# Linear attention, value sums and one rsqrt chain moved between ScalarE, GpSimd and VectorE in an attention kernel

## The chip, the cores and the metric

One core of a Trainium2 chip runs the whole program. The metric is the time of one execution on the device in microseconds (us).

## The reference, cut to what matters

For each of 32 batches (256 tokens, 128 channels, 16 heads of 8 channels) an input is normalised, turned into q, k and v, and two kinds of attention are mixed. The first keeps only the 12 largest softmax weights of each row and divides by their sum; the second is linear attention on softmax features of q and k.

```
xn = layernorm(x);  q, k, v = heads(xn @ Wqkv.T + bqkv);  q, k = layernorm(q), layernorm(k)
aw  = softmax(q @ k.T / sqrt(8));  aws = aw where aw >= the 12th largest, else 0
o_s = (aws / (aws.sum + 1e-8)) @ v
qf, kf = softmax(q over its 8 channels), softmax(k over its 8 channels)
o_l = (qf @ (kf.T @ v)) / (qf . kf.sum + 1e-6)
o   = sigmoid(alpha) * o_s + (1 - sigmoid(alpha)) * o_l
y   = x + (o @ Wproj.T + bproj) + (xn @ W[idx] + b[idx])
```

## The kernel before, in words

Each engine has an instruction stream of its own, written out by hand; semaphores tie them together. Every stream is a loop `body(it, par, xr)` over `it` from -2 to 33, and in it a loop over eight **units** `u_`. A unit is two heads: four tiles of 128 queries by 256 keys. A batch passes through several iterations: its input is normalised and q and k computed in iteration `it` = batch - 2, their normalisation and the transfer into the layout for the scores happen one iteration later, its eight units follow in its own iteration, and its result leaves two iterations later. So every iteration works for up to five batches at once. The order of the work on an engine is the order of the `if u_ == ...` pieces in its body, and nothing else.

The chain of one unit g is this. TensorE makes the scores (`score_ps`, L816). VectorE takes the nine largest positions by `largest` (L532, eight values a tile into `top`). GpSimd subtracts the maximum (`drop`, L364). ScalarE makes the exponentials `e` and their sum `z` (L717) and those of the eight largest (`e8`, L722). In the next unit VectorE removes these eight (`remove`, L539, reads `e8`) and finds the next eight (`following`, L545). In the unit after that GpSimd compares the tiles of `e` with the threshold (`below`, L386), and ScalarE does the tiles that `POOL_TILES` leaves over (L730). TensorE transposes `e` and masks what lies below (`turn`, L834 and L835), ScalarE copies it out (`kept`, L687), TensorE multiplies by v (`product`, L855), and ScalarE copies this (`oT`, L739). `score_ps` has two buffers, so scores wait for the exponentials two units back.

VectorE has six places for extra work in each unit, called `extra(u_, k)`, between those four removals and four searches:

```
remove(0) extra(0) remove(1) extra(1) following(0) extra(2) remove(2) extra(3)
following(1) extra(4) remove(3) following(2) extra(5) following(3)
```

Two of these extras are divisions of results that TensorE leaves in PSUM. In unit 3 the linear part `work_ps` (L951) is multiplied by the reciprocal `lin_z` of its ninth column (L560, L563) into `lin`. In unit 5 the gathered value sums in `pv_ps` (`sums`, L866) are multiplied by the reciprocal of `den` (L579, L584, L587) into `o_sparse`. `product` of unit 6 writes `pv_ps` again and waits for this.

Two rsqrt chains run on ScalarE (`rsqrt_steps`, Ln, Identity, Exp, Square) with a Newton step on GpSimd (`refine`, three instructions): one on 64 columns for q and k in unit 1, one on two columns for the input in unit 2 (ScalarE, L667 to L673) and unit 4 (GpSimd, L329 to L333, then `x_shift`). The feature exponentials of q and of k are two instructions (L758), because q carries the score scale and k none.

The normalised q and k are split into three bf16 parts, which ScalarE copies out of `work_ps` in unit 4 (L701, L751) and unit 5 (L751, `part` 2). The SP queue writes each part to DRAM as it comes (`part_slots`), waits for all, and loads the slots for the next batch in four DMAs (L274), first those of units 0 to 3. TensorE's scores for unit 0 of the next batch, issued in unit 7, wait for the first two of these.

## Time and profile before

| what | value |
|---|---|
| three runs, median (lowest to highest) | 1230.13 us (1228.34 to 1232.35) |
| the profiled execution, its own time | 1228.88 us |
| its span in the trace | 1226.5 us |
| granted TensorE clock over the span | 0.976 |
| VectorE (DVE) busy | 1187.3 us, 97% |
| ScalarE (ACT) busy | 1086.7 us, 89% |
| GpSimd (POOL) busy | 1083.7 us, 88% |
| TensorE (PE) busy | 962.0 us, 78% |

The busy time of an engine is the union of its instructions, counted from the trace; the durations of neighbouring instructions overlap a little, so the price of one that stands in a row is the distance from its start to the start of the next. The profiled execution's own time is 2.4 us above its span.

### The profile page before, as it was taken

The page shows a single profiled execution, that of the slowest core. Times are in us where ns is not written, and L with a number is a line of the kernel's source. Part 1 is how long each engine was busy: PE and PEld are TensorE (multiplying, and loading weights), DVE is VectorE, ACT ScalarE, POOL GpSimd, SP SyncE. Part 2 cuts the span into 40 slices and gives each one's busy share as a digit, 9 for nine tenths or more (in the row PEclk, how much of TensorE's full clock was granted, in tenths as well). Part 3 has the DMA queues.
Part 4 walks back from the last instruction along what each step waited for, and adds up shares of the span by engine and source line. Part 5 has one row for each costly group of instructions (what it writes and reads, how often), then busy time and mean ns, then how long its engine had stood idle before and what let it go on. Part 6 is the DMA issues. An engine that isn't in the chain of part 4 may idle for free.

```text
span 1226.5 us, 34671 instructions
## 1 busy us (share of the span) xinstructions
PE 962.0 (78%) x8997; PEld 653.9 (53%) x9028; DVE 1187.3 (97%) x4553; ACT 1086.7 (89%) x3626; POOL 1083.7 (88%) x1688
## 2 busy tenths in 40 slices
PE   2577878877788788788787878778887888788786
PEld 1255555555556555565555555555555555555554
DVE  6699999999999999999999999999999999999994
ACT  2498999999999999999999989999999999999984
POOL 4599999999999999999999999999999999999964
PEclk9999999999999999989999999999999999999989
DMA  2122212222221222221222221222222122222110
GB/s 62 48 74 79 83 46 65 61 80 83 83 70 43 67 70 83 83 79 41 71 60 83 83 84 45 66 58 83 83 83 65 50 66 71 83 83 79 38 52 14
DMA packets 165143, 82.78 MB, mean 67 GB/s; under 512 B 7753, under 2 KB 164943, under 8 KB 164946
## 3 DMA queue, kind: packets, MB, share of 16 engines
q1 hardware_dynamic: 164946, 80.56, 22.9%
q8 instruction: 74, 1.21, 0.4%
q14 instruction: 123, 1.01, 0.3%
HBM read 42.78 MB, written 37.75 MB: 66 GB/s over the span
## 4 chain that ended last, share of the span: by engine, by line
DVE 60%; issue 26%; PE 4%; DVEq 4%; POOL 3%; ACT 2%; SPq 0%; DMA 0%; POOLq 0%; ACTq 0%
DVE rest L539 26%; DVE top L532 20%; DVE next L545 8%; DVEq L75 4%; POOL below L386 2%; PE turn_ps L834 1%; DVE o_sparse L587 1%; ACT e L717 1%; DVE lin_z L560 1%; DVE den L584 1%; PE pv_ps L855 0%; PE turn_ps L835 0%; DVE stats L595 0%; PE work_ps L932 0%; DVE den L579 0%
## 5 line engine op out<-in xcount | busy, mean ns | idle before, releaser
L386 POOL TENSOR_SCALAR below<-e,next 128x256 bf16<-128x256 f32 x800 | 725.8, 925 | 0.5 <-issue 0.4
L717 ACT ACTIVATE e<-score_ps,drop 128x256 f32<-128x256 f32 x1024 | 472.9, 481 | 57.1 <-POOL drop L364 53.8
L834 PE MATMUL turn_ps<-ident,e 128*128 128x128 f32 x2048 | 401.0, 289 | 40.6 <-ACT kept L687 17.8
L539 DVE MATCH_REPLACE8 rest<-e 128x256 f32<-128x256 f32 x1024 | 409.7, 402 | 0.0
L545 DVE MAX8 next<-rest 128x8 f32<-128x256 f32 x1024 | 403.1, 406 | 0.6 <-issue 0.3
L835 PE MATMUL turn_ps<-minus_huge,below 128*128 128x128 bf16 x2048 | 380.1, 225 | 0.0
L532 DVE MAX8 top<-score_ps 128x8 f32<-128x256 f32 x1024 | 358.4, 408 | 6.8 <-PE score_ps L816 6.6
L834 PEld LDWEIGHTS turn_ps<-ident,e 128*128 128x128 f32 x2048 | 297.6, 145 | 78.9 <-issue 33.0
L687 ACT ACTIVATE kept<-turn_ps 128x1024 f32<-128x1024 f32 x256 | 267.8, 1046 | 39.3 <-PE turn_ps L835 38.9
L835 PEld LDWEIGHTS turn_ps<-minus_huge,below 128*128 128x128 bf16 x2048 | 222.3, 109 | 0.8 <-issue 0.2
L717 ACT ACTIVATION_READ_ACCUMULATOR e<-score_ps,drop 128x1 f32 x1024 | 217.4, 212 | 0.0
L855 PE MATMUL pv_ps<-kept,v_aug 128*32 128x256 f32 x2048 | 143.2, 399 | 1.2 <-ACT out_sb L763 0.9
L816 PE MATMUL score_ps<-k_slots,q_slots 64*128 64x256 bf16 x1024 | 103.3, 279 | 15.2 <-issue 9.1
L364 POOL TENSOR_TENSOR drop<-top 128x36 f32<-128x36 f32 x256 | 63.2, 247 | 58.0 <-DVE top L532 56.9
L730 ACT ACTIVATE below<-e,next 128x256 bf16<-128x256 f32 x224 | 108.0, 516 | 0.0
L855 PEld LDWEIGHTS pv_ps<-kept,v_aug 128*32 128x32 f32 x2048 | 55.6, 113 | 48.2 <-issue 28.0
L932 PE MATMUL work_ps<-w_qk,xnT 128*128 128x256 f32 x128 | 46.8, 449 | 31.9 <-ACT xnT L779 31.9
L816 PEld LDWEIGHTS score_ps<-k_slots,q_slots 64*128 64x128 bf16 x1024 | 30.8, 94 | 74.9 <-issue 67.2
L539 DVE MATCH_VALUE_LOAD rest<-e 128x8 f32 x1024 | 68.1, 66 | 0.8 <-ACT e L722 0.8
L722 ACT ACTIVATE e<-drop 128x32 f32<-128x32 f32 x256 | 63.3, 247 | 0.0
L866 PE MATMUL pv_ps<-gather,oT 128*128 128x128 f32 x256 | 35.0, 280 | 31.9 <-ACT oT L739 31.9
L951 PE MATMUL work_ps<-kv,qfT 128*128 128x144 f32 x128 | 25.4, 323 | 38.9 <-DVE kv L553 38.9
(156 smaller groups left out, 1333.2 us busy)
## 6 DMA issues: line engine op xcount, KB each, us to landing
part_slots<-part SPq DMA_DIRECT2D x128, 192.0 KB, 2.3
q_slots<-part_slots SPq DMA_DIRECT2D x64, 256.0 KB, 3.3
k_slots<-part_slots SPq DMA_DIRECT2D x64, 256.0 KB, 4.1
part_slots<-part SPq DMA_DIRECT2D x64, 128.0 KB, 1.9
x_sb<-in_L_attn_x SPq DMA_DIRECT2D x32, 128.0 KB, 4.2
x_res<-in_L_attn_x SPq DMA_DIRECT2D x32, 128.0 KB, 4.1
out_y<-out_sb SPq DMA_DIRECT2D x32, 128.0 KB, 4.4
w_ops<-in_L_ffn_W SPq DMA_DIRECT2D x1, 512.0 KB
```

The source lines that it names most:

```text
L386: nc.gpsimd.tensor_scalar(below[:, r, t, :], e[:, r, t, :], next8[:, r, t, TOPK - 9:TOPK - 8], None, ALU.is_lt).then_inc(s["below_pool"], 1)
L532: nc.vector.max(top[:, q, t, 1:9], score_ps[:, q, t // 2, t % 2, :]).then_inc(s["top_ready"], 1)
L539: nc.vector.match_replace(rest[:, t, :], e8[:, (u_ - 1) % 2, t, :], e[:, (u_ - 1) % RING, t, :], REMOVED).then_inc(s["rest_ready"], 1)
L545: nc.vector.max(next8[:, (u_ - 1) % RING, t, :], rest[:, t, :]).then_inc(s["next_ready"], 1)
L687: nc.scalar.activation(kept[:, u_ % 4], turn_ps[:], ACT.Relu).then_inc(s["turn_copied"], 1)
L717: nc.scalar.activation(e[:, u_ % RING, t, :], score_ps[:, u_ % 2, t // 2, t % 2, :], ACT.Exp, bias=drop[:, u_ % 2, t, 0:1], accum_out=z[:, ...
L722: nc.scalar.activation(e8[:, u_ % 2], drop[:, u_ % 2, :, 1:9], ACT.Exp).then_inc(s["e8_ready"], 1)
L730: nc.scalar.activation(below[:, r, t, :], e[:, r, t, :], ACT.Relu, scale=-1.0, bias=next8[:, r, t, TOPK - 9:TOPK - 8]).then_inc(s["below_a ...
L816: last = mm(score_ps[:, v_ % 2, hh, nt, :], q_slots[rows, side, v_, nt * P:(nt + 1) * P], k_slots[rows, side, v_, :], start=True, stop=True)
L834: mm(dst, e[:, r, t, keys], ident[:], start=True, stop=False, is_transpose=True)
L835: last = mm(dst, below[:, r, t, keys], minus_huge[:], start=False, stop=True)
L855: last = mm(pv_ps[32 * j:32 * (j + 1), 0:N], v_aug[:, side, mc, 4 * q + j, :], kept[:, v_ % 4, j % 2, mc, :], start=(mc == 0), stop=(mc == ...
```

## The change

- The linear part is copied from PSUM to SBUF by ScalarE in unit 3 (`lin_raw`, 288 columns), its reciprocal is taken by VectorE in unit 4 from SBUF, and GpSimd multiplies in unit 4.
- The value sums are copied by ScalarE in unit 5 (`sums_sb`, 288 columns). GpSimd makes the denominator in unit 6 (two instructions), VectorE its reciprocal in unit 7, GpSimd multiplies in unit 7. TensorE's `product` of unit 6 now waits for the copy.
- One rsqrt chain of 66 columns in unit 1 takes the place of the two. VectorE's statistics of the input move from unit 1 to unit 0, and the load of the input one iteration ahead.
- q and k both carry 8^(-1/4), so that one exponential of 512 columns makes both features.
- `POOL_TILES` goes from (3, 2, 3, 4, 4, 4, 3, 2) to (3, 2, 4, 3, 4, 3, 3, 2), its first entry being unit 2: GpSimd does one tile more in unit 4, one less in units 5 and 7; ScalarE the reverse.

```diff
 SHARE_MIN = 1e-20
 Z_EPS = 1e-6
-SCORE_SCALE = float(1.0 / np.sqrt(np.float32(D)))
+SIDE_SCALE = float(np.float32(D) ** -0.25)
 UNITS = H // 2
...
 SLOTS_OF = ((slice(0, 3), slice(3, 6), slice(6, 8)), (slice(0, 8, 3), slice(1, 8, 3), slice(2, 8, 3)))
 ROWS = len(SLOTS) * D
-POOL_TILES = (3, 2, 3, 4, 4, 4, 3, 2)
+POOL_TILES = (3, 2, 4, 3, 4, 3, 3, 2)
 POOL_SUM = sum(POOL_TILES)
...
-                if exists(it + 2) and not (isinstance(it, int) and it < 0):
-                    wait_alone(sp, s["xn_ready"], NT * (it + 1), s["waits_passed"])
-                    sp.dma_start(x_sb[:, par], x_t[it + 2]).then_inc(x_loaded[par], 16)
+                if exists(it + 3) and not (isinstance(it, int) and it < -1):
+                    wait_alone(sp, s["xn_ready"], NT * (it + 2), s["waits_passed"])
+                    sp.dma_start(x_sb[:, nxt], x_t[it + 3]).then_inc(x_loaded[nxt], 16)
                 if exists(it - 2):
...
-            def refine(rsqrt, kind, n):
-                v, r, half, out = (rsqrt[:, i] for i in range(4))
-                nc.gpsimd.tensor_tensor(half, half, v, ALU.mult).then_inc(s[kind + "_newton"], 1)
-                wait_alone(pool, s[kind + "_newton"], n + 1, s["waits_passed"])
-                nc.gpsimd.tensor_scalar(half, half, -1.0, 1.5, ALU.mult, ALU.add).then_inc(s[kind + "_newton"], 1)
-                pool.wait_ge(s[kind + "_newton"], n + 2)
-                nc.gpsimd.tensor_tensor(out, r, half, ALU.mult).then_inc(s[kind + "_newton"], 1)
+            def refine(it):
+                lo = 0 if exists(it + 1) else GROUPS
+                hi = GROUPS + NT if exists(it + 2) else GROUPS
+                n = STEPS * (it + 2)
+                v, r, half, out = (rsqrt[:, i, lo:hi] for i in range(4))
+                pool.wait_ge(s["rsqrt_ready"], 2 * (it + 3))
+                nc.gpsimd.tensor_tensor(half, half, v, ALU.mult).then_inc(s["newton"], 1)
+                wait_alone(pool, s["newton"], n + 1, s["waits_passed"])
+                nc.gpsimd.tensor_scalar(half, half, -1.0, 1.5, ALU.mult, ALU.add).then_inc(s["newton"], 1)
+                pool.wait_ge(s["newton"], n + 2)
+                nc.gpsimd.tensor_tensor(out, r, half, ALU.mult).then_inc(s["newton"], 1)
+            def shift(it):
+                n = STEPS * (it + 2)
+                pool.wait_ge(s["newton"], n + 3)
+                nc.gpsimd.tensor_tensor(x_shift[:, 0], moments[:, GROUPS:, 0], rsqrt[:, 3, GROUPS:],
+                                        ALU.mult).then_inc(s["newton"], 1)
+                wait_alone(pool, s["newton"], n + 4, s["waits_passed"])
+                nc.gpsimd.tensor_scalar(x_shift[:, 1], x_shift[:, 0], -1.0, None, ALU.mult).then_inc(s["newton"], 1)
...
+                    if u_ == 6 and exists(it - 1):
+                        wait_alone(pool, s["sums_copied"], it, s["waits_passed"])
+                        nc.gpsimd.tensor_scalar(den[:, 0], z[:, nxt].rearrange("p t h -> p (t h)"), SUM_EPS, None,
+                                                ALU.mult).then_inc(s["den_step"], 1)
+                        pool.wait_ge(s["den_step"], it)
+                        nc.gpsimd.tensor_tensor(den[:, 1], den[:, 0], sums_sb[:, :, D], ALU.add).then_inc(
+                            s["den_ready"], 1)
...
+                    if u_ == 1 and (exists(it + 1) or exists(it + 2)):
+                        refine(it)
...
-                        pool.wait_ge(s["x_rsqrt_ready"], 2 * (it + 3))
-                        n = X_STEPS * (it + 2)
-                        refine(x_rsqrt, "x", n)
-                        pool.wait_ge(s["x_newton"], n + 3)
-                        nc.gpsimd.tensor_tensor(x_shift[:, 0], x_mv[:, :, 0], x_rsqrt[:, 3],
-                                                ALU.mult).then_inc(s["x_newton"], 1)
-                        wait_alone(pool, s["x_newton"], n + 4, s["waits_passed"])
-                        nc.gpsimd.tensor_scalar(x_shift[:, 1], x_shift[:, 0], -1.0, None,
-                                                ALU.mult).then_inc(s["x_newton"], 1)
+                        shift(it)
+                    if u_ == 4 and exists(it):
+                        pool.wait_ge(s["linz_ready"], it + 1)
+                        nc.gpsimd.tensor_tensor(lin[:, par].rearrange("p t (h d) -> p (t h) d", d=D),
+                                                lin_raw[:, :, 0:D],
+                                                lin_z[:].unsqueeze(2).to_broadcast([P, NT * H, D]),
+                                                ALU.mult).then_inc(s["lin_ready"], 1)
...
+                    if u_ == 7 and exists(it - 1):
+                        pool.wait_ge(s["rden_ready"], it)
+                        nc.gpsimd.tensor_tensor(o_sparse[:].rearrange("p t (h d) -> p (t h) d", d=D),
+                                                sums_sb[:, :, 0:D],
+                                                den[:, 2].unsqueeze(2).to_broadcast([P, NT * H, D]),
+                                                ALU.mult).then_inc(s["osp_ready"], 1)
...
-                    if u_ == 3 and k in (1, 3) and exists(it):
-                        w = work_ps[:, 0:NT * H * VA].rearrange("p (t h e) -> p t h e", t=NT, e=VA)
-                        if k == 1:
-                            dve.wait_ge(s["w_lin"], it + 1)
-                            nc.vector.reciprocal(lin_z[:], w[:, :, :, D]).then_inc(s["linz_step"], 1)
-                        if k == 3:
-                            dve.wait_ge(s["linz_step"], it + 1)
-                            nc.vector.tensor_tensor(
-                                lin[:, par].rearrange("p t (h d) -> p (t h) d", d=D),
-                                work_ps[:, 0:NT * H * VA].rearrange("p (g e) -> p g e", e=VA)[:, :, 0:D],
-                                lin_z[:].rearrange("p t h -> p (t h)").unsqueeze(2).to_broadcast([P, NT * H, D]),
-                                ALU.mult).then_inc(s["lin_ready"], 1)
...
-                    if u_ == 5 and 1 <= k <= 4 and exists(it - 1):
-                        w = pv_ps[:, 0:NT * H * VA].rearrange("p (g e) -> p g e", e=VA)
-                        n = 2 * (it - 1)
-                        if k == 1:
-                            dve.wait_ge(s["w_turn"], it)
-                            nc.vector.scalar_tensor_tensor(out=den[:, 0], in0=z[:, nxt].rearrange("p t h -> p (t h)"),
-                                                           scalar=SUM_EPS, in1=w[:, :, D], op0=ALU.mult,
-                                                           op1=ALU.add).then_inc(s["den_step"], 1)
+                    if u_ == 4 and k == 1 and exists(it):
+                        dve.wait_ge(s["lin_copied"], it + 1)
+                        nc.vector.reciprocal(lin_z[:], lin_raw[:, :, D]).then_inc(s["linz_ready"], 1)
+                    if u_ == 7 and k == 1 and exists(it - 1):
+                        dve.wait_ge(s["den_ready"], it)
+                        nc.vector.reciprocal(den[:, 2], den[:, 1]).then_inc(s["rden_ready"], 1)
+                    if u_ == 0 and exists(it + 2):
                         if k == 2:
...
-                            dve.wait_ge(s["den_step"], n + 1)
-                            nc.vector.reciprocal(den[:, 1], den[:, 0]).then_inc(s["den_step"], 1)
-                        if k == 4:
-                            dve.wait_ge(s["den_step"], n + 2)
-                            nc.vector.tensor_tensor(o_sparse[:].rearrange("p t (h d) -> p (t h) d", d=D), w[:, :, 0:D],
-                                                    den[:, 1].unsqueeze(2).to_broadcast([P, NT * H, D]),
-                                                    ALU.mult).then_inc(s["osp_ready"], 1)
-                    if u_ == 1 and exists(it + 2):
-                        if k == 0:
...
+            def rsqrt_steps(it):
+                lo = 0 if exists(it + 1) else GROUPS
+                hi = GROUPS + NT if exists(it + 2) else GROUPS
+                n = it + 2
+                if exists(it + 1):
+                    act.wait_ge(s["ss_ready"], it + 2)
+                if exists(it + 2):
+                    act.wait_ge(s["x_mean"], NT * (it + 3))
+                wait(act, s["newton"], STEPS * n)
+                nc.scalar.activation(log[:, lo:hi], moments[:, lo:hi, 1], ACT.Ln, bias=LN_EPS).then_inc(
+                    s["rsqrt_step"], 1)
+                nc.scalar.activation(rsqrt[:, 0, lo:hi], moments[:, lo:hi, 1], ACT.Identity, bias=LN_EPS).then_inc(
+                    s["rsqrt_ready"], 1)
+                act.wait_ge(s["rsqrt_step"], 2 * n + 1)
+                nc.scalar.activation(rsqrt[:, 1, lo:hi], log[:, lo:hi], ACT.Exp, scale=-0.5).then_inc(
+                    s["rsqrt_step"], 1)
+                act.wait_ge(s["rsqrt_step"], 2 * n + 2)
+                nc.scalar.activation(rsqrt[:, 2, lo:hi], rsqrt[:, 1, lo:hi], ACT.Square,
+                                     scale=float(0.5 ** 0.5)).then_inc(s["rsqrt_ready"], 1)
...
+                    if u_ == 3 and exists(it):
+                        act.wait_ge(s["w_lin"], it + 1)
+                        wait(act, s["lin_ready"], it)
+                        nc.scalar.copy(lin_raw[:].rearrange("p g e -> p (g e)"), work_ps[:, 0:NT * H * VA]).then_inc(
+                            s["lin_copied"], 1)
...
-                            wait(act, s["osp_ready"], it - 1)
+                            wait(act, s["den_ready"], it - 1)
...
+                    if u_ == 5 and exists(it - 1):
+                        act.wait_ge(s["w_turn"], it)
+                        wait(act, s["osp_ready"], it - 1)
+                        nc.scalar.copy(sums_sb[:].rearrange("p g e -> p (g e)"), pv_ps[:, 0:NT * H * VA]).then_inc(
+                            s["sums_copied"], 1)
...
-                        sub = d_sub[:].rearrange("p (t a c) -> p t a c", t=NT, a=2)
-                        for side, dst, factor in ((0, q_exp[:, nxt], 1.0 / SCORE_SCALE), (1, k_exp[:], 1.0)):
-                            nc.scalar.activation(dst, sub[:, :, side, :], ACT.Exp,
-                                                 scale=factor).then_inc(s["dexp_ready"], 1)
+                        nc.scalar.activation(qk_exp[:, nxt].rearrange("p t a c -> p (t a c)"), d_sub[:], ACT.Exp,
+                                             scale=1.0 / SIDE_SCALE).then_inc(s["dexp_ready"], 1)
...
-                        wait(pe, s["osp_ready"], it)
+                        wait(pe, s["sums_copied"], it)
...
-                        wait(pe, s["lin_ready"], it + 1)
+                        wait(pe, s["lin_copied"], it + 1)
```

Names in the rows below: `part` is a bf16 part of q and k, `e` the exponentials, `kept` the masked transpose. **VectorE in unit 5**, before:

```order
L532 MAX top<-score_ps 128x8 [waits scores_ready,drop_ready]
L532 MAX top<-score_ps 128x8 [waits scores_ready] x3
L539 MATCH_REPLACE rest<-e 128x256 [waits e8_ready,next_ready] x2
L579 SCALAR_TENSOR_TENSOR den<-z,pv_ps 128x32 [waits w_turn]
L545 MAX next<-rest 128x8 [waits rest_ready]
L584 RECIPROCAL den<-den 128x32 [waits den_step]
L539 MATCH_REPLACE rest<-e 128x256 [waits e8_ready,next_ready]
L545 MAX next<-rest 128x8 [waits rest_ready]
L587 TENSOR_TENSOR o_sparse<-pv_ps,den 128x256 [waits den_step]
L539 MATCH_REPLACE rest<-e 128x256 [waits e8_ready,next_ready]
L545 MAX next<-rest 128x8 [waits rest_ready] x2
```

and now:

```order
L556 MAX top<-score_ps 128x8 [waits scores_ready,drop_ready]
L556 MAX top<-score_ps 128x8 [waits scores_ready] x3
L563 MATCH_REPLACE rest<-e 128x256 [waits e8_ready,next_ready] x2
L569 MAX next<-rest 128x8 [waits rest_ready]
L563 MATCH_REPLACE rest<-e 128x256 [waits e8_ready,next_ready]
L569 MAX next<-rest 128x8 [waits rest_ready]
L563 MATCH_REPLACE rest<-e 128x256 [waits e8_ready,next_ready]
L569 MAX next<-rest 128x8 [waits rest_ready] x2
```

Three instructions are gone from the unit: the denominator, its reciprocal and the multiplication; the reciprocal comes back in unit 7.

**ScalarE in unit 5, from its exponentials to the v copy of unit 6**, before:

```order
L717 ACTIVATE e,z<-score_ps,drop 128x256 [waits turn_ready,drop_ready]
L717 ACTIVATE e,z<-score_ps,drop 128x256 x3
L722 ACTIVATE e<-drop 128x32
L751 CAST part<-work_ps 128x512 [waits w_rest,next_ready]
L775 ACTIVATE xn<-x_sb,x_shift,x_rsqrt 128x128 [waits w_xT,x_newton]
L775 ACTIVATE xn<-x_sb,x_shift,x_rsqrt 128x128
L687 ACTIVATE kept<-turn_ps 128x1024 [waits turn_ready,pv_ready]
L705 COPY v_aug<-work_ps 128x32x8 [waits w_v_ready]
```

and now:

```order
L731 ACTIVATE e,z<-score_ps,drop 128x256 [waits turn_ready,drop_ready]
L731 ACTIVATE e,z<-score_ps,drop 128x256 x3
L736 ACTIVATE e<-drop 128x32
L744 ACTIVATE below<-e,next 128x256 [waits next_ready]
L760 COPY sums_sb<-pv_ps 128x288 [waits osp_ready,w_turn]
L770 CAST part<-work_ps 128x512 [waits w_rest]
L788 ACTIVATE xn<-x_sb,x_shift,rsqrt 128x128 [waits w_xT,newton]
L788 ACTIVATE xn<-x_sb,x_shift,rsqrt 128x128
L698 ACTIVATE kept<-turn_ps 128x1024 [waits turn_ready,pv_ready]
L719 COPY v_aug<-work_ps 128x32x8 [waits w_v_ready]
```

A `below` tile and the copy of the sums now stand ahead of the last part, of `xn` and of `kept`.

**GpSimd from the start of unit 4 to the start of unit 5**, before:

```order
L364 TENSOR_TENSOR drop<-top 128x36 [waits top_ready,e8_ready]
L386 TENSOR_SCALAR below<-e,next 128x256 [waits next_ready] x3
L329 TENSOR_TENSOR x_rsqrt<-x_rsqrt 128x2 [waits x_rsqrt_ready]
L331 TENSOR_SCALAR x_rsqrt<-x_rsqrt 128x2 [waits x_newton]
L333 TENSOR_TENSOR x_rsqrt<-x_rsqrt 128x2 [waits x_newton]
L402 TENSOR_TENSOR x_shift<-x_mv,x_rsqrt 128x2 [waits x_newton]
L405 TENSOR_SCALAR x_shift<-x_shift 128x2 [waits x_newton]
L364 TENSOR_TENSOR drop<-top 128x36 [waits top_ready,e8_ready]
```

and now:

```order
L372 TENSOR_TENSOR drop<-top 128x36 [waits top_ready,e8_ready]
L402 TENSOR_SCALAR below<-e,next 128x256 [waits next_ready] x4
L340 TENSOR_TENSOR x_shift<-moments,rsqrt 128x2 [waits newton]
L343 TENSOR_SCALAR x_shift<-x_shift 128x2 [waits newton]
L419 TENSOR_TENSOR lin<-lin_raw,lin_z 128x256 [waits linz_ready]
L372 TENSOR_TENSOR drop<-top 128x36 [waits top_ready,e8_ready]
```

The three Newton instructions of the input are gone, one tile and the multiplication of the linear part have come.

## Rows read from the trace of the kernel before

**Rows 1.** Waits (all engines): engine, line, releaser: us in total, times, longest.

```profile
POOL drop L364 <- DVE top L532: 56.9, 99, 6.6
...
DVE den L579 <- PE pv_ps L866: 11.7, 2, 11.0
...
PE score_ps L816 <- issue: 9.1, 13, 1.4
```

**Rows 2.** Stretch of one batch, all engines: busy us (count), clock.

```profile
602.90:639.25 36.35, 28.86 (x283) 19.85 (x283) 36.35 (x141) 33.87 (x114) 33.63 (x53) 1.00 0.25 71
```

**Rows 3.** Timeline, VectorE, starts of units 5 to 0 and extras: start, us, instruction.

```profile
573.99 1.40 DVE L532 MAX8 top<-score_ps 128x8 f32<-128x256 f32 x4
...
576.10 0.17 DVE L579 SCALAR_TENSOR_TENSOR den<-z,pv_ps 128x32 f32<-128x32 f32 x1
576.19 0.41 DVE L545 MAX8 next<-rest 128x8 f32<-128x256 f32 x1
...
577.45 0.40 DVE L587 TENSOR_TENSOR o_sparse<-pv_ps,den 128x256 f32<-128x256 f32 x1
577.78 0.07 DVE L539 MATCH_VALUE_LOAD rest<-e 128x8 f32 x1
...
578.83 1.40 DVE L532 MAX8 top<-score_ps 128x8 f32<-128x256 f32 x4
...
583.25 1.39 DVE L532 MAX8 top<-score_ps 128x8 f32<-128x256 f32 x4
...
587.45 0.73 DVE L532 MAX8 top<-score_ps 128x8 f32<-128x256 f32 x2
```

**Rows 4.** Costliest groups, VectorE: count, busy us, mean ns of one.

```profile
L563 DVE TENSOR_TENSOR lin<-work_ps,lin_z 128x256 f32<-128x256 f32 x32 | 13.0, 407 | 0.0
...
L560 DVE RECIPROCAL lin_z<-work_ps 128x32 f32<-128x32 f32 x32 | 10.9, 341 | 0.0
...
L604 DVE RECIPROCAL k_rec<-k_sum 128x32 f32<-128x32 f32 x32 | 10.5, 328 | 3.8 <-POOL k_sum L415 3.8
```

**Rows 5.** Timeline, GpSimd, units 4 and 5.

```profile
574.30 0.20 POOL L329 TENSOR_TENSOR x_rsqrt<-x_rsqrt 128x2 f32<-128x2 f32 x1
...
575.25 0.20 POOL L402 TENSOR_TENSOR x_shift<-x_mv,x_rsqrt 128x2 f32<-128x2 f32 x1
...
575.84 0.24 POOL L364 TENSOR_TENSOR drop<-top 128x36 f32<-128x36 f32 x1
576.07 3.64 POOL L386 TENSOR_SCALAR below<-e,next 128x256 bf16<-128x256 f32 x4
```

**Rows 6.** Costliest groups, GpSimd.

```profile
L351 POOL TENSOR_TENSOR qkn<-qk_b,beta 128x512 f32<-128x512 f32 x32 | 40.7, 1271 | 0.1
...
L422 POOL TENSOR_TENSOR k_feat<-k_exp,k_rec 128x256 f32<-128x256 f32 x32 | 20.3, 634 | 0.5 <-DVE k_rec L604 0.5
```

**Rows 7.** Timeline, ScalarE, units 4 to 6.

```profile
573.61 0.52 ACT L730 ACTIVATE below<-e,next 128x256 bf16<-128x256 f32 x1
574.01 0.38 ACT L739 COPY oT<-pv_ps 128x256 f32<-128x256 f32 x1
574.26 0.61 ACT L751 CAST part<-work_ps 128x512 bf16<-128x512 f32 x1
...
576.27 0.51 ACT L717 ACTIVATE e<-score_ps,drop 128x256 f32<-128x256 f32 x1
...
578.18 0.65 ACT L751 CAST part<-work_ps 128x512 bf16<-128x512 f32 x1
...
580.34 0.44 ACT L705 COPY v_aug<-work_ps 128x256 f32<-128x256 f32 x1
```

**Rows 8.** Timeline, TensorE, the scores of a unit 0 that came latest.

```profile
732.41 0.60 PE L816 MATMUL score_ps<-k_slots,q_slots 64*128 64x256 bf16 x4 [1.45 <-issue]
```

**Rows 9.** Timeline, VectorE, the unit 0 that needed them.

```profile
733.18 1.43 DVE L532 MAX8 top<-score_ps 128x8 f32<-128x256 f32 x4
```

**Rows 10.** One line, VectorE, within one batch: duration ns min/median/max.

```profile
L539 DVE MATCH_REPLACE8 rest<-e x33: 395/397/407, 566.2 to 602.6; 128x256 f32<-128x256 f32 x33
```

92 lines of the change are left out of this document (38 added, 54 removed).

## The prediction

> **What bounds the kernel now.** Start with the stretch of one batch: 36.35 us from one batch to the next, and VectorE is busy for all 36.35 of them, ScalarE for 33.87, GpSimd for 33.63 [rows 2]. 32 batches of 36.35 are 1163 of the 1226.5 us of the span. Then the waits: GpSimd waits for VectorE's `top` in 99 places, 56.9 us in all, while VectorE itself has one long wait, 11.0 us at the very end [rows 1]. So VectorE sets the pace, and an instruction taken from it shortens every batch, as long as nothing behind it becomes late. The timeline of VectorE gives the unit lengths: unit 5 takes 4.84 (573.99 to 578.83), unit 6 4.42, unit 7 4.20 [rows 3]. The third thing to see is thin cover. TensorE waited 13 times before scores with no engine named, up to 1.4 us [rows 1]. These are unit 0's scores, waiting for the slot loads; in the worst case they start at 732.41 and end at 733.01, and VectorE begins that unit at 733.18 [rows 8, 9]. Today this costs nothing, by 0.17 us.
>
> **What VectorE loses, part by part.** `o_sparse` goes: 577.45 to 577.78 is 0.33 us. `den` goes: 576.10 to 576.19 is 0.09 [rows 3]. `lin` goes; it has the same form and duration (407 ns against 0.40 us) [rows 3, 4], so 0.33. Both reciprocals stay. That of the linear part now reads SBUF; the one that reads PSUM takes 341 ns, one that reads SBUF 328 [rows 4], so 0.01, which I take as 0.4 us over the run. Statistics and their aggregation only change unit. Together 0.33 x 32 for `lin`, 0.42 x 31 for the sums (the last batch's stand in the tail), and 0.4: **24.0 us less**. A batch would take 35.6.
>
> The Trainium skill (VectorE: DVE Perf Modes, "The TRN2 errata") gives VectorE a fixed part of 58 cycles from SBUF and 120 from PSUM at 0.96 GHz. By that the reciprocal would gain 65 ns, an estimate, 2 us over the run instead of 0.4. The trace disagrees in size.
>
> **What GpSimd gets.** In each batch it loses one tile, 3.64 / 4 = 0.91, and three Newton instructions, 574.30 to 575.25 = 0.95 [rows 5]. It gets two multiplications of 256 columns. The nearest row is `k_feat` with 0.63; the upper bound is 1.27, the costliest row of two inputs, which has 512 columns [rows 6]; the lower is 0.33, what VectorE pays. The inputs now step by 9, not 8, but that is close to `k_feat`, so 0.63 each. It also gets two small instructions on 32 columns for the denominator, between 0.2 each (the smallest row) and 0.63; I take 0.7 for both with the wait between them. Sum: 1.96 more, 1.86 less, so +0.1. Of its 36.35 it spends 33.63 busy, about 1.3 in gaps between its own dependent instructions, and the rest waiting for VectorE. 34.9 + 0.1 = 35.0 fits into 35.6. On average GpSimd doesn't bind.
>
> **What ScalarE gets.** Two copies of 288 columns: one of 256 costs 574.01 to 574.26 = 0.25, so 0.28 each. One tile more: 573.61 to 574.01 = 0.40 [rows 7]. It loses the four small activations of the input's chain, each between nothing and the 0.25 of the copy, so 0 to 1.0; with one exponential less I take 0.7 for all of it. Sum: +0.3, 34.2 of 35.6. Also hidden on average.
>
> **Where it gets tight: unit 5.** Place by place, from the start T5 of VectorE's unit 5. Before: GpSimd's `drop` at +1.85 [rows 5], ScalarE's exponentials at +2.28, last `part` at +4.19, v copy at +6.35 [rows 7], unit 0 of the next batch at +13.46 [rows 3]. Now:
> - GpSimd's unit 4 grows by 0.91 + 0.63 - 0.95 = 0.59, VectorE's by 0.25 (the moved reciprocal), so `drop` comes 0.34 later. ScalarE was 0.16 later still than `drop` allowed; a unit 4 without tile leaves it early enough. The exponentials start at +2.48, 0.20 later.
> - Tile and copy of the sums stand ahead of the last `part`: 0.40 + 0.28. It is cast at +5.07, **0.88 later**.
> - Unit 0 comes at +13.04, because unit 5 is 0.64 shorter and unit 7 is 0.22 longer by its reciprocal: **0.42 earlier**.
>
> On the SP queue nothing passes anything, but the last part's two writes and the four slot loads wait for this cast. So the slack between slot loads and unit 0 shrinks by 1.30. In the 13 late cases, read from the two timelines as in the one that is shown, it was 0.17 to 1.36, 11.3 us in sum. 13 x 1.30 - 11.3 = **5.6 us** of new stalls: VectorE waits for unit 0's scores. In the other batches TensorE's scores are done 1.7 ahead, and nothing is lost. The bounds are 0 (the loads get out of each other's way, as the input's load is a batch ahead now) and 11 (as many more cases come into reach).
>
> The second thin place is `product` of unit 6. It waited for `o_sparse`; now it waits for the copy of the sums, which ends at 2.48 + 1.91 + 0.40 + 0.38 = +5.2. From the product to the v copy took 2.3, so v is copied at +7.5 and unit 6's exponentials start at +7.8. They take 2.05 with `e8`, and VectorE removes with `e8` 1.33 after the start of unit 7, at +9.95. Margin 0.1. I put 1 us for the batches that miss it; bounds 0 and 5.
>
> **The tail.** After the last sums the chain was three VectorE instructions, 1.0 us (`den` 0.17, reciprocal 0.33, `o_sparse` 0.40 and two hops). Now it is the copy (0.38), GpSimd twice (0.7), reciprocal (0.33), GpSimd (0.63): 2.1 with its hops. GpSimd ends its tiles one earlier but has a multiplication more. +1.0. At the start the chain that ends last runs over VectorE's setup, unchanged: 0.
>
> **Sum.** 1228.9 (own time of the profiled execution) - 24.0 + 5.6 + 1.0 + 1.0 = **1212.5 us**. The median of the runs, 1230.1, is 0.1% above the profiled one; I leave the number at 1212.5.
>
> **The rivals.**
> - *Nothing stalls:* the slot loads still arrive. 1228.9 - 24.0 + 1.0 = 1206. For it: the input load moved ahead; the late cases are less than half. Against: 13 of them are there already and the cast is later by the sum of rows above.
> - *Unit 6 misses `e8` in every batch.* If ScalarE or TensorE is 0.3 later than worked out, VectorE loses 0.3 x 32 = 9 us more: 1221. For it: a margin of 0.1 on a path of five engines. Against: every price on it stands in a row.
> - *GpSimd becomes the bound, slower than before.* The place is its multiplications with inputs that step by 9. It decides from 35.6 - 35.0 = 0.6 us a batch, and the gain is gone at 1.3, which is where each costs as much as 512 columns (1.27 against 0.63). With the denominator at its upper bound besides (+0.5) a batch takes 36.8: 1228.9 + 0.45 x 32 + 1 = 1244. Against: `k_feat` at 0.63 has a broadcast input too.
> - *GpSimd's reads hold VectorE up.* MATCH_REPLACE takes 395 to 407 ns within one batch [rows 10], in which GpSimd works for 33.63 of 36.35 [rows 2]. If it did hold it up, the new 1.26 a batch would come back as waits of VectorE: 1228.9 - 24 + 40 + 1 = 1246. The rows show nothing like it. The Trainium skill (Perfetto Trace Analysis, "Optimizing Scalar/DVE Operations") warns of just this: both share an SBUF read port, so moving operations between them might not help. The Trainium skill (SBUF — State Buffer, "Who interferes with whom") limits it to VectorE instructions with two SBUF inputs or in a two-port mode; so far the trace agrees, since those of this kernel are not held up.
> - *The change doesn't take work from VectorE:* excluded, the order of instructions shows three fewer a batch.
>
> **How the numbers follow.** Forecast (5 to 12 us of stalls and tail) 0.47; nothing stalls 0.22; `e8` missed 0.16; slower through GpSimd 0.06, through the port 0.02; what I don't see, from no gain to a small loss, 0.07. A measurement of this kernel tells 0.3%, 3.7 us. Faster by more than that: 0.47 + 0.22 + 0.15 = 0.84, since a missed `e8` could take more than I priced; the same 0.01 of that and 0.06 of the unseen, 0.07; slower 0.06 + 0.02 + 0.01 = 0.09. The range goes from 1204 (nothing stalls, tail at nothing) to 1224 (the stalls at both upper bounds); it leaves out 0.2.
>
> **What would show it.** In the changed profile: two copies of 288 columns on ScalarE at about 0.38; VectorE's unit 5 at 4.20; `lin` and `o_sparse` on GpSimd at 0.63; `part` 2 cast 5.1 after T5; a batch of 35.6 where nothing stalls, and VectorE waiting for `score_ps` in some batches. Wrong: multiplications above 0.9; GpSimd no longer waiting for `top`; waits of VectorE for ScalarE's `e8` in every batch; or units of VectorE that grow without a wait.

## The result and the profile after

| | median | runs, lowest to highest |
|---|---|---|
| before | 1229.89 us | 20 runs, 1227.97 to 1232.74 |
| changed | 1222.3 us | 20 runs, 1216.27 to 1228.83 |

The ratio is 0.9939, 95% interval [0.9924, 0.9954]: faster by 0.6%, 7.6 us. Forecast were 1212.5 and a gain of 17. The direction was right and the range (1204 to 1224) holds the time, but less than half of the gain arrived. The profiled execution took 1221.65 us, its span 1219.9.

**The waits of the changed kernel** answer to [rows 1]. Columns: engine, line, releaser, us in total, times, longest.

```profile
PE pv_ps L869 <- ACT sums_sb L760: 55.6, 31, 2.0
POOL drop L372 <- DVE top L556: 52.0, 92, 7.2
...
DVE top L556 <- PE score_ps L830: 12.9, 14, 6.3
DVE den L591 <- POOL den L391: 12.0, 1, 12.0
DVE rest L563 <- ACT e L736: 4.8, 14, 0.6
```

GpSimd still waits for VectorE's `top`, as before. New are the first row, in which TensorE stands before `product` of unit 6 in 31 of the 32 batches, and the last: VectorE waits for ScalarE's `e8`. The `top` row holds 6.3 us at the start of the program; 6.6 us of it lie in the batches.

**One quiet batch**, all engines (busy us and count of PE, PEld, DVE, ACT, POOL, then clock, DMA share, GB/s), beside [rows 2]:

```profile
400.08:435.83 35.75, 28.49 (x279) 19.55 (x278) 35.68 (x138) 33.98 (x114) 33.79 (x53) 1.00 0.25 73
```

35.75, not 35.6: VectorE has 0.07 of idle time by this count, and its first remove of unit 7 comes 0.15 late. **The timeline of VectorE** in it, beside [rows 3]:

```profile
422.63 1.41 DVE L556 MAX8 top<-score_ps 128x8 f32<-128x256 f32 x4
...
426.84 1.41 DVE L556 MAX8 top<-score_ps 128x8 f32<-128x256 f32 x4
...
431.26 1.40 DVE L556 MAX8 top<-score_ps 128x8 f32<-128x256 f32 x4
432.73 0.09 DVE L563 MATCH_VALUE_LOAD rest<-e 128x8 f32 x1
```

Unit 5 takes 4.21 (predicted 4.20), unit 6 4.42. The first remove of unit 7 starts 1.47 after the unit, where it needs 1.33. **ScalarE's timeline**, beside [rows 7]:

```profile
425.10 0.47 ACT L731 ACTIVATE e<-score_ps,drop 128x256 f32<-128x256 f32 x1 [0.55 <-POOL drop L372]
...
427.02 0.52 ACT L744 ACTIVATE below<-e,next 128x256 bf16<-128x256 f32 x1
427.42 0.41 ACT L760 COPY sums_sb<-pv_ps 128x288 f32<-128x288 f32 x1
427.70 0.62 ACT L770 CAST part<-work_ps 128x512 bf16<-128x512 f32 x1
...
430.23 0.37 ACT L719 COPY v_aug<-work_ps 128x256 f32<-128x256 f32 x1 [0.23 <-PE work_ps L935]
430.50 0.48 ACT L731 ACTIVATE e<-score_ps,drop 128x256 f32<-128x256 f32 x1
```

and **TensorE's** `product` behind the copy, then its scores of the next unit 0 (an engine's wait stands in brackets behind its row):

```profile
427.97 1.07 PE L869 MATMUL pv_ps<-kept,v_aug 128*32 128x256 f32 x16 [1.73 <-ACT sums_sb L760]
...
435.22 0.40 PE L830 MATMUL score_ps<-k_slots,q_slots 64*128 64x256 bf16 x4 [0.33 <-issue]
```

From T5 = 422.63, measured (predicted): exponentials +2.47 (+2.48), last part +5.07 (+5.07), copy of the sums ended +5.20 (+5.2), product +5.34 (+5.2), v copy +7.60 (+7.5), exponentials of unit 6 +7.87 (+7.8), VectorE's first remove +10.10 (wanted +9.95). **GpSimd's groups** (count, busy us, mean ns), beside [rows 6]:

```profile
L419 POOL TENSOR_TENSOR lin<-lin_raw,lin_z 128x256 f32<-128x256 f32 x32 | 20.2, 630 | 0.0
...
L438 POOL TENSOR_TENSOR o_sparse<-sums_sb,den 128x256 f32<-128x256 f32 x32 | 20.1, 628 | 0.5 <-DVE den L591 0.5
```

Both multiplications cost what `k_feat` costs, and units 0 to 6 of VectorE have the same lengths in nearly all batches (4.72, 4.21, 4.42, 4.80, 4.41, 4.21, 4.42).

**Where the rest went.** Unstalled, units 6 and 7 take 8.82 together. Over 31 batches they took 16.7 us more than that, read from the starts of VectorE's units. 7.4 of these are waits for `e8`: about 0.15 in most batches, 0.25 to 0.68 in eleven. The other 9.3 stand before unit 0. (The list of waits puts down 4.8 and 6.6; it leaves the smallest out.) In six batches TensorE's scores of unit 0 waited with no engine named, which is the slot loads:

```profile
292.22 0.40 PE L830 MATMUL score_ps<-k_slots,q_slots 64*128 64x256 bf16 x4 [1.07 <-issue]
```

These six are worth 3.5 us. The largest cases, 1.6 us of the two kinds together in each of four batches, show another thing. **TensorE in one of them:**

```profile
572.45 1.07 PE L869 MATMUL pv_ps<-kept,v_aug 128*32 128x256 f32 x16 [1.89 <-ACT sums_sb L760]
...
578.58 1.16 PE L946 MATMUL work_ps<-w_qk,xnT 128*128 128x256 f32 x2
...
581.20 0.40 PE L830 MATMUL score_ps<-k_slots,q_slots 64*128 64x256 bf16 x4
```

**the stretches around it, TensorE** (busy us and count, granted clock, DMA share, GB/s):

```profile
571.00:572.00 1.00, 0.00 (x0) 1.00 0.00 0
572.00:573.00 1.00, 0.55 (x12) 1.00 0.00 0
573.00:574.00 1.00, 1.00 (x15) 0.97 0.21 65
574.00:575.00 1.00, 1.00 (x6) 0.50 0.70 198
...
580.00:581.00 1.00, 1.00 (x4) 0.62 1.10 328
581.00:582.00 1.00, 1.00 (x11) 1.00 0.43 126
```

**and VectorE:**

```profile
575.79 1.43 DVE L556 MAX8 top<-score_ps 128x8 f32<-128x256 f32 x4
577.59 0.09 DVE L563 MATCH_VALUE_LOAD rest<-e 128x8 f32 x1 [0.38 <-ACT e L736]
...
581.79 1.10 DVE L556 MAX8 top<-score_ps 128x8 f32<-128x256 f32 x3 [1.01 <-PE score_ps L830]
```

TensorE stood for 1.89 us, worked again, and then the granted clock fell to 0.50, from 574 to 580.8. That is the lower of its two levels, 1.2 GHz, as the Trainium skill has them (TensorE: Matmul & The Clock Gate, "What's actually happening"; the trace agrees in that it shows 1.00 and 0.50 of the full clock). TensorE, busy in every slice at that level, needs 5.41 us from the start of VectorE's unit 7 to the scores of unit 0, against 3.96 in the quiet batch (435.22 after 431.26), and VectorE waits. Of the 16.7 us, then: 7.4 for `e8`, 3.5 for slot loads, about 5 for scores that come late in batches with a low clock, and 0.8 that I don't assign.

**The tail.** After the last value sums TensorE waits for `o_sparse` before it gathers it. Kernel before, then changed kernel:

```profile
1220.38 0.33 PE L894 MATMUL pv_ps<-ident,o_sparse 128*128 128x128 f32 x1 [1.12 <-DVE o_sparse L587]
```

```profile
1211.94 0.33 PE L908 MATMUL pv_ps<-ident,o_sparse 128*128 128x128 f32 x1 [2.41 <-POOL o_sparse L438]
```

The wait is 1.3 us longer, near the +1.0 of the forecast. But from there to the end of the program it takes 7.98 us instead of 6.15, since the granted clock is 0.52 in this stretch and was 1.00 before. From the start of VectorE's last unit to the end the changed kernel takes 28.5 us, against 25.4.

### The profile page after: what moved, and what is told of

It reads as the page before. It is cut to its first block, busy times and chain, and to the rows that moved or that the text cites. A ratio compares the mean times of both kernels' runs of the same rounds, so it can differ in the third digit from the quotient of the medians.

```text
span 1219.9 us, 34490 instructions
## 1 busy us (share of the span) xinstructions
PE 964.7 (79%) x8997; PEld 659.4 (54%) x9028; DVE 1166.8 (96%) x4457; ACT 1094.1 (90%) x3566; POOL 1090.5 (89%) x1691
## 4 chain that ended last, share of the span: by engine, by line
DVE 33%; ACT 23%; issue 20%; PE 13%; POOL 8%; DVEq 2%; DMA 1%; SPq 0%; POOLq 0%; ACTq 0%
ACT e L731 13%; DVE rest L563 13%; DVE top L556 11%; POOL below L402 6%; DVE next L569 4%; PE pv_ps L869 3%; ACT kept L698 2%; PE work_ps L934 2%; PE turn_ps L848 2%; DVEq L75 2%; ACT below L744 1%; PE work_ps L946 1%; PE turn_ps L849 1%; ACT e L736 1%; PE work_ps L935 1%
## 5 line engine op out<-in xcount | busy, mean ns | idle before, releaser
L402 POOL TENSOR_SCALAR below<-e,next 128x256 bf16<-128x256 f32 x768 | 695.7, 922 | 0.1
L848 PE MATMUL turn_ps<-ident,e 128*128 128x128 f32 x2048 | 399.4, 289 | 34.4 <-ACT kept L698 16.7
L563 DVE MATCH_REPLACE8 rest<-e 128x256 f32<-128x256 f32 x1024 | 419.0, 414 | 0.3 <-issue 0.3
L569 DVE MAX8 next<-rest 128x8 f32<-128x256 f32 x1024 | 412.0, 416 | 0.4 <-issue 0.3
L698 ACT ACTIVATE kept<-turn_ps 128x1024 f32<-128x1024 f32 x256 | 271.1, 1059 | 32.0 <-PE turn_ps L849 31.6
L731 ACT ACTIVATION_READ_ACCUMULATOR e<-score_ps,drop 128x1 f32 x1024 | 228.8, 223 | 0.0
L869 PE MATMUL pv_ps<-kept,v_aug 128*32 128x256 f32 x2048 | 138.9, 389 | 56.9 <-ACT sums_sb L760 55.6
L744 ACT ACTIVATE below<-e,next 128x256 bf16<-128x256 f32 x256 | 128.4, 531 | 0.0
L563 DVE MATCH_VALUE_LOAD rest<-e 128x8 f32 x1024 | 82.2, 80 | 6.0 <-ACT e L736 4.8
L753 ACT COPY oT<-pv_ps 128x256 f32<-128x256 f32 x128 | 51.9, 406 | 1.3 <-PE pv_ps L869 1.3
```

The source lines that it names most:

```text
L402: nc.gpsimd.tensor_scalar(below[:, r, t, :], e[:, r, t, :], next8[:, r, t, TOPK - 9:TOPK - 8], None, ALU.is_lt).then_inc(s["below_pool"], 1)
L563: nc.vector.match_replace(rest[:, t, :], e8[:, (u_ - 1) % 2, t, :], e[:, (u_ - 1) % RING, t, :], REMOVED).then_inc(s["rest_ready"], 1)
L569: nc.vector.max(next8[:, (u_ - 1) % RING, t, :], rest[:, t, :]).then_inc(s["next_ready"], 1)
L698: nc.scalar.activation(kept[:, u_ % 4], turn_ps[:], ACT.Relu).then_inc(s["turn_copied"], 1)
L731: nc.scalar.activation(e[:, u_ % RING, t, :], score_ps[:, u_ % 2, t // 2, t % 2, :], ACT.Exp, bias=drop[:, u_ % 2, t, 0:1], accum_out=z[:, ...
L744: nc.scalar.activation(below[:, r, t, :], e[:, r, t, :], ACT.Relu, scale=-1.0, bias=next8[:, r, t, TOPK - 9:TOPK - 8]).then_inc(s["below_a ...
```

## The experiments

Edits are relative to the changed kernel where nothing else is said. Theory A was: what counts is when `product` of unit 6 starts. Theory B was the one of the prediction: the last part is cast late, and the slot loads with it. Code cuts are marked with `...`.

**The copy of the sums early.** It moves in ScalarE's unit 5 from behind `e8` and the tile to a place ahead of the exponentials, right behind `kept`.

```diff
+                    if u_ == 5 and exists(it - 1):
+                        act.wait_ge(s["w_turn"], it)
+                        wait(act, s["osp_ready"], it - 1)
+                        nc.scalar.copy(sums_sb[:].rearrange("p g e -> p (g e)"), pv_ps[:, 0:NT * H * VA]).then_inc(
+                            s["sums_copied"], 1)
                     if u_ == 3 and exists(it):
...
-                    if u_ == 5 and exists(it - 1):
-                        act.wait_ge(s["w_turn"], it)
-                        wait(act, s["osp_ready"], it - 1)
-                        nc.scalar.copy(sums_sb[:].rearrange("p g e -> p (g e)"), pv_ps[:, 0:NT * H * VA]).then_inc(
-                            s["sums_copied"], 1)
```

> The changed kernel, with ScalarE's copy of the value sums moved from behind unit 5's exponentials and tile to ahead of them, right behind `kept`. Theory A (TensorE's product of unit 6 stands 1.8 us a batch waiting for this copy, and everything behind it, v copy, unit 6's exponentials, the next batch's scores, comes that much later and reaches VectorE in unit 7): the wait of product for sums_sb goes, VectorE's unit 7 goes back from 4.58 to 6.0 us to 4.42, total 1207 to 1211 us, and the runs lie close together. Theory B (the recorded one: the last part is cast too late and the slot loads with it): the part comes only 0.3 us earlier, total 1218 to 1221 us, spread as wide as now.

Measured 1206.71 us (1206.0 to 1209.29), ratio 0.9806 [0.9788, 0.9825]. That is 0.3 below A's range, and 11 below B's. The wait for `sums_sb` is gone from TensorE, and a batch takes what was predicted for one that doesn't stall:

```profile
397.48:433.06 35.58, 31.34 (x282) 21.49 (x281) 35.58 (x138) 33.41 (x110) 33.88 (x53) 0.91 0.26 75
```

This batch has a stretch of low clock too (0.91 on average), and it costs nothing. So low clock by itself is not yet a loss; it becomes one where TensorE's work has no cover left.

**The last part first.** The opposite: the last part's cast goes ahead of the tile and of the copy, which makes the slot loads earlier and the product later.

```diff
+                    if u_ == 5 and exists(it + 1):
+
+                        p = u_ - 3
+                        act.wait_ge(s["w_rest"], 2 * (it + 1) + p)
+                        nc.scalar.copy(part[:, p], work_ps[:].rearrange("p (a n) -> p a n", a=2)).then_inc(
+                            s["part_ready"], 1)
                     if exists(it if u_ >= 2 else it - 1):
...
-                    if u_ in (4, 5) and exists(it + 1):
+                    if u_ == 4 and exists(it + 1):
```

> The changed kernel, with unit 5's cast of the last part moved ahead of the `below` tile and of the copy of the sums; the copy comes 0.5 us later. Theory A: TensorE waits 0.5 us longer, unit 7 grows by that in every batch, total 1232 to 1238 us. Theory B: the slot loads come 0.7 us earlier, the waits for scores go, total 1215 to 1218 us.

Measured 1260.33 us (1259.41 to 1261.91), ratio 1.0240 [1.0221, 1.0258]. Right in sign, but the loss against the changed kernel is 38 us, more than twice what A allowed. Waits of VectorE:

```profile
DVE top L556 <- PE score_ps L836: 41.3, 43, 6.3
...
DVE rest L563 <- ACT e L736: 12.9, 32, 0.6
```

The waits for `e8` explain 15 us; the larger part is the wait for scores, in batches with low clock. This is where the clock became part of the theory.

**The sums back on VectorE.** Copy, denominator and multiplication of the sums are undone; the linear part stays moved.

```diff
-                    if u_ == 7 and k == 1 and exists(it - 1):
...
+                    if u_ == 5 and 1 <= k <= 4 and exists(it - 1):
...
-                        wait(pe, s["sums_copied"], it)
+                        wait(pe, s["osp_ready"], it)
```

> The changed kernel with the value sums divided on VectorE in unit 5 as before (no copy, no GpSimd steps for them); linear part, rsqrt chain, exponential and tiles stay changed. VectorE has 0.42 us a batch more. Theory A: product waits for VectorE's o_sparse, not for ScalarE, no excess in unit 7, total 1230 - 24 + 13 = about 1219 us, and the runs within 3 us of each other. Theory B: the part comes 0.3 us earlier and unit 5 is 0.4 longer, most late batches covered, total 1222 us or more.

Measured 1215.47 us (1214.97 to 1217.02), ratio 0.9872 [0.9853, 0.9892], 3.5 below A's 1219; the narrow spread is as A had it. The half of the change that takes 0.42 us a batch off VectorE makes the program 7 us slower than leaving it out. VectorE's batch is 36.01 here, as the sum has it (36.35 less the 0.33 for `lin`).

**The old table of tiles**, without and with the early copy.

```diff
-POOL_TILES = (3, 2, 4, 3, 4, 3, 3, 2)
+POOL_TILES = (3, 2, 3, 4, 4, 4, 3, 2)
```

> The changed kernel with the tiles shared as before the change (GpSimd 4 in unit 5, 3 in unit 4, 4 in unit 7), so that no tile stands ahead of the copy in unit 5. Theory A: the copy and the product come 0.4 us earlier and unit 7's excess goes, but GpSimd has 0.9 us a batch more (about 35.9 against VectorE's 35.6), total 1212 to 1219 us. Theory B: the part is 0.4 us earlier too, but only the batches with late slot loads gain; with GpSimd's part 1220 to 1226 us. If GpSimd were the bound already, 1240 us or more.

> The early copy with the tiles shared as before the change: GpSimd has one tile, 0.9 us, a batch more, about what the merged rsqrt chain took from it. By the sum of rows GpSimd needs 35.9 a batch against VectorE's 35.6: total 1215 to 1220 us if it is the bound then; 1207 to 1209 if it has more room than the rows say.

Measured 1229.69 us (1226.68 to 1231.9), ratio 0.9991 [0.9979, 1.0003], and with the early copy 1226.45 (1224.22 to 1231.4), 0.9980 [0.9968, 0.9992]. Both expectations missed. The wait for the sums is shorter without the tile ahead of it, and yet the gain is gone. Waits of TensorE, with the early copy:

```profile
PE pv_ps L908 <- ACT oT L758: 50.3, 29, 2.2
```

It was 25.2 us, at most 1.0, in the changed kernel. So TensorE stands elsewhere: before the gathering of `o_sparse` and `lin` at the end of unit 1. What follows one of these stands, TensorE and then the stretches of all engines:

```profile
227.78 0.30 PE L908 MATMUL pv_ps<-ident,o_sparse 128*128 128x128 f32 x1 [2.10 <-ACT oT L758]
```

```profile
228.00:229.00 1.00, 1.00 (x8) 0.32 (x6) 1.00 (x6) 1.00 (x3) 1.00 (x2) 0.55 0.00 0
229.00:230.00 1.00, 1.00 (x6) 0.95 (x4) 1.00 (x5) 0.97 (x6) 1.00 (x3) 0.50 0.03 8
```

and VectorE, whose unit 2 takes 5.38 instead of 4.42 (230.55 to 235.93):

```profile
230.55 1.40 DVE L556 MAX8 top<-score_ps 128x8 f32<-128x256 f32 x4
235.93 1.42 DVE L556 MAX8 top<-score_ps 128x8 f32<-128x256 f32 x4 [0.79 <-PE score_ps L830]
```

It is the same pattern in another place, but not the whole difference. The 31 batches take 18.4 us more than with the early copy alone: 10.8 in unit 2, nearly all of it in 16 batches in which the clock falls, 2.9 in unit 3, 4.6 in units 6 and 7. GpSimd has a tile more a batch in this table, and TensorE's transposes wait 19.3 us for its `below`, against 6.2. No run separates what of the 18.4 is due to GpSimd's load and what to the clock.

**The linear part back on VectorE**, with the early copy.

```diff
+                    if u_ == 3 and k in (1, 3) and exists(it):
...
-                        nc.scalar.copy(lin_raw[:].rearrange("p g e -> p (g e)"), work_ps[:, 0:NT * H * VA]).then_inc(
-                            s["lin_copied"], 1)
...
```

> The early copy with the linear part divided on VectorE in unit 3 as before the change. VectorE gets 0.33 us a batch back, a multiplication of 256 columns: 1206.7 + 10.6 = 1217 us, in steady batches of 35.9. If VectorE weren't the bound, less.

Measured 1218.82 us (1216.17 to 1220.08), ratio 0.9912 [0.9896, 0.9929], 12.1 above the early copy. The 10.6 of the sum (0.33 x 32) stand, within the spread of the runs.

**Copy early and last part early:** the first two edits together. This is the one that moves the cast, relative to the early copy:

```diff
+                    if u_ == 5 and exists(it + 1):
+
+                        p = u_ - 3
+                        act.wait_ge(s["w_rest"], 2 * (it + 1) + p)
+                        nc.scalar.copy(part[:, p], work_ps[:].rearrange("p (a n) -> p a n", a=2)).then_inc(
+                            s["part_ready"], 1)
                     if exists(it if u_ >= 2 else it - 1):
...
-                    if u_ in (4, 5) and exists(it + 1):
+                    if u_ == 4 and exists(it + 1):
```

> The changed kernel with the copy of the sums ahead of unit 5's exponentials (as in the early copy) and also the last part cast ahead of unit 5's tile, 0.4 us earlier. Theory A: VectorE no longer waits in the steady batches, so there is nothing left to gain: 1206 to 1208 us. Theory B (late slot loads cost something): 3 to 6 us below the early copy, 1201 to 1204 us.

Measured 1204.84 us (1204.71 to 1205.05), ratio 0.9801 [0.9785, 0.9817]. No wait of VectorE for scores is left but the one at the start (6.3 us, one time). It is the lowest of all times, and its runs don't overlap those of the early copy, though the intervals of the ratios do. The time lies between A's range (1206 to 1208) and B's (1201 to 1204): by this the late slot loads cost the early copy some 2 us. The cast that costs 38 us in one order is harmless in another.

**The copy half as early.** Behind `e8`, ahead of the tile; the last part and all behind it stay where they are.

```diff
                         nc.scalar.activation(e8[:, u_ % 2], ...).then_inc(s["e8_ready"], 1)
+                    if u_ == 5 and exists(it - 1):
+                        act.wait_ge(s["w_turn"], it)
+                        wait(act, s["osp_ready"], it - 1)
+                        nc.scalar.copy(sums_sb[:].rearrange("p g e -> p (g e)"), pv_ps[:, 0:NT * H * VA]).then_inc(
+                            s["sums_copied"], 1)
                     if exists(it if u_ >= 2 else it - 1):
```

> The changed kernel with ScalarE's copy of the sums one step earlier, between e8 and the tile of unit 5; last part, xn and kept stay where they are. Theory A (the start of product of unit 6 counts, through two costs: the chain to e8, and the stretches in which TensorE's granted clock falls to half): product starts at T5 + 4.9 instead of 5.3, the wait for the sums falls from 1.8 to 1.4 us a batch, the chain has its margin of 0.25 back, units 6 and 7 come to 8.82 again but for batches with a late slot load (some 4 us of the 16.7). 1208 to 1212. Theory B (what costs is the late last part, by its slot loads): nothing that matters moves, 1218 to 1224.

Measured 1213.17 us (1209.32 to 1214.21), ratio 0.9862 [0.9839, 0.9885]. TensorE's and VectorE's waits:

```profile
PE pv_ps L870 <- ACT sums_sb L741: 43.1, 31, 1.6
...
DVE rest L563 <- ACT e L736: 1.4, 4, 0.5
```

0.4 us earlier, and the waits for `e8` are gone from nearly all batches. The late slot loads stay, as A had it, at 5.9 us before unit 0 instead of its 4; the time is 1.2 above A's range.

**The early copy with a wait put in.** The order of ScalarE stays that of the early copy; `product` alone is held back, first to the cast of the last part, then to `xn`.

```diff
                         wait(pe, s["sums_copied"], it)
+                        if exists(it + 1):
+                            pe.wait_ge(s["part_ready"], PARTS * (it + 2))
```

```diff
                         wait(pe, s["sums_copied"], it)
+                        if exists(it + 2):
+                            pe.wait_ge(s["xn_ready"], NT * (it + 3))
```

> The kernel with the early copy of the sums (1206.7), but product of unit 6 waits in addition for the cast of the last part, which puts it at T5 + 5.3 to 5.4, where it starts in the changed kernel; ScalarE's order stays as in the early copy. Theory A: the gain of the early copy goes, 1218 to 1226, with unit 7 above 4.5 in most batches and some long stretches of low clock. Rival (the early copy gained by what ScalarE does, not by when product starts): 1206 to 1209.

> As the run before, but product of unit 6 waits for xn of unit 5, T5 + 5.8 to 5.9, where it starts when the last part is cast first. Theory A: as with the last part first, 1250 to 1262, about 2 us for each batch, and a long stretch of low clock in most batches. Rival (with the last part first it was ScalarE's order that cost the 38 us): 1212 to 1230, the chain's 0.4 to 0.5 late a batch and no more.

Measured 1241.47 us (1236.11 to 1247.36), ratio 1.0099 [1.0061, 1.0137], and 1267.99 us (1263.75 to 1272.23), 1.0325 [1.0285, 1.0364]. Both are above A's price; the product came at +5.52 and +6.30, later than I had it. The rivals (ScalarE's order is what counts) fall. First kernel, then second:

```profile
PE pv_ps L871 <- ACT part L770: 60.6, 31, 2.1
DVE top L556 <- PE score_ps L830: 20.8, 23, 6.3
```

```profile
PE pv_ps L871 <- ACT xn L788: 82.6, 30, 2.8
...
DVE top L556 <- PE score_ps L830: 43.5, 31, 6.3
```

**The kernel before, with a wait put in.** Nothing of the change; `product` waits for `xn`, then for GpSimd's first pair sum of k's exponentials.

```diff
                         wait(pe, s["osp_ready"], it)
+                        if exists(it + 2):
+                            pe.wait_ge(s["xn_ready"], NT * (it + 3))
```

```diff
                         wait(pe, s["osp_ready"], it)
+                        if exists(it + 1):
+                            pe.wait_ge(s["ksum_step"], 2 * (it + 1) + 1)
```

> The kernel before with one wait more: TensorE's product of unit 6 also waits for ScalarE's xn of unit 5, which it doesn't use. TensorE stands about 1.6 us there in each batch, as it does in the changed kernel. Theory A1 (only the length of the chain counts): by the rows of before unit 6's exponentials would still come 0.2 us before VectorE needs them and unit 0's scores too, total 1230 to 1233 us. Theory A2 (the standing lowers TensorE's granted clock in the stretch behind it, and the slow matmuls make the chain late): low-clock stretches of 6 us behind the wait in a third or more of the batches, mean clock 0.96 or less, total 1236 to 1255 us, wide spread.

> The kernel before; product of unit 6 waits in addition for GpSimd's first pair sum of k's exponentials in unit 5, T5 + 6.1 instead of 4.0, 2.1 us of standing (0.5 more than with the wait for xn, which cost 1.8 us in all and lowered no clock). Theory C (a stand of TensorE of about 2 us is what the drop of the granted clock follows): long stretches of low clock in over half of the batches, and 1250 or more. Theory D (the clock falls only where work after the stand is in a hurry as well; the stand alone doesn't do it): e8 is missed by 0.2 to 0.4 in each batch, 1234 to 1243, with under 6 stretches of low clock.

Measured 1231.88 us (1229.59 to 1233.48), ratio 1.0017 [1.0008, 1.0027], and 1264.23 us (1261.94 to 1265.06), 1.0280 [1.0261, 1.0299]. First kernel, then second:

```profile
PE pv_ps L857 <- ACT xn L775: 48.2, 30, 1.7
```

```profile
PE pv_ps L857 <- POOL k_half L415: 65.8, 31, 2.4
```

A stand of 1.6 us cost 2 us in all, as theory A1 had it, and the loss lies in the first batch (its units 6 and 7 took 7.08 and 5.14); A2, low clock by this stand, missed: the mean clock was 0.992, above the 0.976 of the kernel before. One of 2.17 costs 34. In the second, one of the stands and the stretches behind it, TensorE:

```profile
294.54 1.94 PE L857 MATMUL pv_ps<-kept,v_aug 128*32 128x256 f32 x16 [2.17 <-POOL k_half L415]
```

```profile
292.00:293.00 1.00, 0.37 (x5) 1.00 0.00 0
293.00:294.00 1.00, 0.00 (x0) 1.00 0.00 0
294.00:295.00 1.00, 0.47 (x8) 0.73 0.87 246
295.00:296.00 1.00, 1.00 (x16) 0.50 0.06 16
```

The product itself takes 1.94 here, against 1.07. The clock fell for a long stretch in nine batches, whose unit 6 took 5.62 to 5.99 us; where it stood at 1.00 after the same stand, unit 6 took 4.41 to 4.54 in all batches but the first. So C's time came and its count (over half) was too high; D's time and count both missed. D's idea, that the clock falls only where the work behind the stand is in a hurry as well, is not settled: with 2.17 us every batch is late for `e8` too, with 1.6 hardly any is. Shown is that the wait alone brings the lateness and the low clock: no other instruction was changed.

**All of them in one table.** Product and wait are the usual value within a batch; extra is what units 6 and 7 took over their unstalled length in the 31 batches of the profiled execution, and its part for `e8`; long is the number of batches in which the clock stood at 0.50 for six or more of the 1 us slices between the start of unit 6 and unit 0.

| kernel | product at | its wait | extra, us | of it `e8` | long | profiled run, us |
|---|---|---|---|---|---|---|
| copy early | +3.39 | none | 1.0 | 0.7 | 0 | 1206.11 |
| copy half as early | +4.93 | 1.49 | 5.9 | 0.0 | 0 | 1212.14 |
| changed | +5.34 | 1.89 | 16.7 | 7.4 | 4 | 1221.65 |
| early, waits for part | +5.52 | 2.07 | 31.4 | 12.7 | 12 | 1236.11 |
| last part first | +5.84 | 2.38 | 55.1 | 15.2 | 23 | 1261.22 |
| early, waits for `xn` | +6.30 | 2.84 | 58.7 | 17.7 | 14 | 1263.75 |

From row to row the extra and the run's own time grow by the same amounts: 1206.11 - 1.0 = 1205.1, 1221.65 - 16.7 = 1205.0, 1263.75 - 58.7 = 1205.1, the others 1204.7 to 1206.2. So what sets these kernels apart lies in units 6 and 7. In the last row the batches with a long stretch cost more (2.74 us each over the unstalled length, against 2.15 in the row above).

## Where the prediction was right, and which steps failed

**VectorE's 24.0 us less, the tail's +1.0: right in sum, partly by luck.** The base 1205.0 of the table is the time without any stall in units 6 and 7, and 1228.9 - 24.0 + 1.0 = 1206 was the forecast of that case. The batch of the early copy is 35.58 (predicted 35.6), and undoing `lin` alone gave 12.1 back (predicted 10.6). But without those stalls the way from VectorE's first unit to its last is 26 us shorter, not 24, and the tail is 3.1 us longer, not 1.0: 1.3 for the chain that was worked out, 1.8 for the low clock behind it. The two misses nearly cancel.

**GpSimd, ScalarE, the ports: right.** 630 and 628 ns a multiplication (predicted 634); the copies came at 0.28 us from start to start (427.42 to 427.70). With GpSimd at 89% busy VectorE's unit 6 still took 4.42. (The durations of its instructions in this trace are 12 ns longer, 414 against 402 for MATCH_REPLACE, but 406 in the early copy, in which GpSimd does the same work.) The Trainium skill warns that moving work between the two might not help (Perfetto Trace Analysis, "Optimizing Scalar/DVE Operations"). That didn't come true here: the early copy is 23 us below the kernel before.

**The slot loads, +5.6 us: right in kind, 3.5 measured.** The cast was 0.88 later, as worked out. But six batches stalled, not 13; why fewer wasn't tried. The reading that the latest case of before costs nothing, by 0.17 us, was wrong: VectorE starts 0.18 us behind the end of the scores in the stalled batches of the changed kernel too, so this is the hop from TensorE to VectorE and no slack, and unit 7 ahead of that case took 4.41 us instead of 4.20.

**The margin of 0.1 before `e8`: the first step that failed.** I priced it at 1.0 us, at most 5; it was 7.4. The places were right to 0.01 as far as the end of the copy (+5.20). But `product` starts 0.14 behind that end, and I let it start at once; the exponentials of unit 6 come 0.07 later than worked out; and VectorE starts 2.23 behind their start, not 2.05, since the hop from `e8` to VectorE (0.17) was left out as well. 0.07 and 0.18 make 0.25, and the margin was not +0.1 but -0.15: missed in nearly every batch. That is the rival "unit 6 misses `e8` in every batch", which had a chance of 0.16 and the time 1221; it came true in its place, at half of its price a batch (0.15 instead of 0.3). That its 1221 is so near to the measured time is luck: the rest of the loss came from the next step.

**TensorE's clock: a term that the prediction put at nothing.** It reads the 1.9 us that TensorE stands before `product` as a delay of what follows, and nothing more. Shown is that the stand has a second price: in the kernel before, where a wait was put in and nothing else changed, 1.6 us cost 2 us over the program and 2.17 us cost 34. Less than half of it is at `e8` (15.4), which a delay alone explains; the rest is at scores, most of it in the batches in which the granted clock was at 0.50 behind the stand. In the changed kernel this was some 5 us before unit 0, and part of the 7.4 at `e8` as well (0.47 a batch instead of 0.15). Its mark was in the profile of before: the clock of 0.976 over the span, at which VectorE still didn't wait in the batches but for the late slot loads.

**The sum by what was measured:** 1228.9 - 24.0 + 1.0 (tail) + 16.7 = 1222.6 against 1221.65 of the profiled execution. The stalls of 6.6 in the forecast were 16.7; that term is the whole miss.

**The range** went to 1224, called the stalls at both upper bounds. By its own terms these give 1228.9 - 24.0 + 1.0 + 11 + 5 = 1221.9, with the profiled run (1221.65) just inside and the median (1222.3) just outside. That the range holds the time is due to this slip of 2 us.

Left open is what decides whether the clock falls after a stand. With the same 1.89 us it fell for long in 4 batches of 31 and not in the others, and in the kernel before and the early copy it falls at times with no such stand ahead of `product`. I didn't find what sets these batches apart.

## What to carry to other kernels

When an operation moves off the busiest engine, put its copy where the engine that needs the buffer next doesn't have to stand for it; here one place in ScalarE's order was worth 15.6 us, twice the whole gain of the change. Work a thin margin out with the hop between engines at each step (0.14 to 0.18 us here), and if it comes out within one hop of nothing, price the miss in every batch. And when TensorE is made to stand longer, look at the granted clock of the microseconds behind the stand, not only at the wait.

## What the runs showed of the hardware

- The granted clock of one TensorE falls to half in some batches and not in others of the same program, after stands of equal length. The time of the changed kernel follows it from run to run: 1216.27 us at a mean clock of 0.984, 1222.21 at 0.971, 1228.83 at 0.954. The spread is 12.6 us, against 4.8 for the kernel before, so a single run of such a kernel says little. The early copy and last part together spread by 0.34 (5 runs).
- In these kernels the low clock costs only what lies uncovered behind it: the profiled run of the early copy had a clock of 0.975, that of the copy half as early 0.983, and the first was faster by 6.0 us (1206.11 against 1212.14).
- A table of tiles that gives GpSimd one tile more a batch cost 20 us with the early copy (1226.45 against 1206.71), more than half of it in unit 2, behind a stand of TensorE at another place.
- In the tail of all ten kernels in which GpSimd makes `o_sparse`, TensorE stands for 2.4 us, and the granted clock of the last 7.5 to 8.2 us is 0.50 to 0.60. Where VectorE makes it, the stand is 1.1 us and the clock 1.00, except in the kernel before with the longer wait put in (0.64).
